# Splitting the selection over experts in two halves, moving the label row's product into the v product, and taking the low part of the log gates forward

## The reference

```
q2 = (x @ Wqa @ Wqb).reshape(B, L, H, DK) * scale
k2 = softmax((x @ Wka @ Wkb).reshape(B, L, H, DK), axis=-1)
gk1 = (log_sigmoid(x @ Wg1a @ Wg1b + bg1) / NORMALIZER).reshape(B, L, H, DK)
gk2 = (log_sigmoid(x @ Wg2a @ Wg2b + bg2) / NORMALIZER).reshape(B, L, H, DK)
e = softmax(x @ We, axis=-1)
_, idx = lax.top_k(e, 1)
mask = one_hot(idx, N_EXP).sum(-2)          # one expert per row
...
o_dense = gla_b(q1, k1, v, gk1)
o_sparse = gla_be(q_e, k_e, v, gk_e).sum(axis=1)
o = o_dense + o_sparse                      # gla: chunks of 64 rows, a running state per head
```

## Time and profile before

| | |
|---|---|
| median of 3 runs | 2540.27 us (2538.45 to 2542.61) |
| the profiled execution's own time | 2541.0 us |
| its span, first to last instruction | 2539.2 us |
| second pass, start of one step's `cumulate` to the next | 30.32 us |
| TensorE busy | 95% of the span |
| VectorE busy | 70% of the span |

### The profile page before, as it was taken

The page is one execution under the profiler, slowest core; times in us unless marked ns, Lnnn a source line. Parts: engine busy times, 40 slices in busy tenths (PEclk is TensorE's granted clock), DMA queues, the critical chain, the costliest instruction groups (busy, mean ns, idle before and its releaser), DMA issues.

```text
span 2539.2 us, 56360 instructions
## 1 busy us (share of the span) xinstructions
PE 2412.6 (95%) x20208; PEld 1423.8 (56%) x20208; DVE 1770.0 (70%) x3484; ACT 1562.6 (62%) x3281; POOL 1194.1 (47%) x929
## 2 busy tenths in 40 slices
PE   4999999998999999999999999999999999999997
PEld 2444444454666565666666665656666666666554
DVE  4444544426777777777777777777777777777775
ACT  3222323236777777777776777777777767777763
POOL 1797332214444444445544454444454444444444
PEclk9999999999999999999999999999999999999999
DMA  6434444311111111111111111111111111111111
GB/s 215 103 100 131 102 106 108 83 49 32 43 45 41 41 41 41 41 45 46 45 45 42 45 42 42 41 41 41 45 45 49 42 44 43 41 41 41 41 25 34
DMA packets 250704, 145.65 MB, mean 57 GB/s; under 512 B 208096, under 2 KB 208096, under 8 KB 250144
## 3 DMA queue, kind: packets, MB, share of 16 engines
q1 hardware_dynamic: 240048, 119.32, 18.8%
q10 hardware_dynamic: 9504, 17.31, 1.8%
q0 software_dynamic: 1104, 8.40, 0.9%
HBM read 61.09 MB, written 33.55 MB: 37 GB/s over the span
## 4 chain that ended last, share of the span: by engine, by line
PE 79%; DVE 13%; issue 4%; POOL 3%; DMA 1%; ACT 1%; DVEq 0%; POOLq 0%; SPq 0%; ACTq 0%
PE psum L319 17%; PE psum L320 16%; PE psum L321 16%; PE psum L583 6%; DVE region L1217 6%; PE psum L447 5%; PE psum L437 4%; PE psum L464 4%; PE psum L331 2%; DVE region L1214 2%; PE psum L456 2%; PE psum L418 2%; PE psum L367 1%; PE psum L419 1%; PE psum L368 1%
## 5 line engine op out<-in xcount | busy, mean ns | idle before, releaser
L1053 POOL TENSOR_TENSOR region<-region,kfac 128x512 f32<-128x512 f32 x64 | 124.4, 1944 | 379.4 <-DVE kfac L1304 379.4
L319 PE MATMUL psum<-wb,region 128*128 128x512 f16 x768 | 293.1, 382 | 0.0
L320 PE MATMUL psum<-wb,region 128*128 128x512 f16 x768 | 292.1, 380 | 0.0
L321 PE MATMUL psum<-wb,region 128*128 128x512 f16 x768 | 292.1, 380 | 0.0
L1036 POOL TENSOR_TENSOR region<-region 128x1024 f32<-128x1024 f32 x64 | 147.8, 2310 | 266.0 <-DVE region L1408 233.3
L1408 DVE SCALAR_TENSOR_TENSOR region<-psum,region 128x512 f16<-128x512 f32 x64 | 44.3, 692 | 225.3 <-ACT region L865 225.3
L1041 POOL TENSOR_TENSOR region<-region 128x1024 f32<-128x1024 f32 x64 | 150.8, 2356 | 105.3 <-DVE region L1183 105.3
L1048 POOL TENSOR_SCALAR region<-region,m 128x512 f32<-128x512 f32 x256 | 172.4, 693 | 34.8 <-DVE hm L1254 34.8
L583 PE MATMUL psum<-region 128*128 128x512 f16 x768 | 176.2, 379 | 2.1 <-DVE region L1408 2.1
L1081 POOL TENSOR_TENSOR og<-og 128x512 f16<-128x512 f32 x64 | 74.1, 1158 | 190.9 <-ACT og L807 190.9
L1217 DVE SCALAR_TENSOR_TENSOR region<-psum,m,region 128x512 f32<-128x512 f32 x192 | 144.2, 751 | 6.8
(11 more groups left out here) (232 smaller groups left out, 7204.2 us busy)
## 6 DMA issues: line engine op xcount, KB each, us to landing
region<-x_in SPq DMA_DIRECT2D x128, 256.0 KB, 2.6
q_cols<-region ACTq DMA_DIRECT2D x64, 256.0 KB, 2.5
region<-q_cols SPq DMA_DIRECT2D x64, 256.0 KB, 2.8
out_rows<-region SPq DMA_DIRECT2D x62, 256.0 KB, 2.0
region<-wb_in POOLq DMA_DIRECT2D x1, 3072.0 KB, 11.6
region<-wqkv_in SPq DMA_DIRECT2D x4, 512.0 KB, 6.0
region<-region SPq DMA_TRANSPOSE x128, 3.0
region<-ws_in POOLq DMA_DIRECT2D x1, 1280.0 KB, 15.7
```

Source lines behind the costliest of these rows:

```text
L319: mm(out, lhs(0), rhs(0), start=start, stop=False)
L320: mm(out, lhs(0), rhs(1), start=False, stop=False)
L321: return mm(out, lhs(1), rhs(0), start=False, stop=stop)
L1053: nc.gpsimd.tensor_tensor(kd.rearrange("p (h d) -> p h d", h=H2), kd.rearrange("p (h d) -> p h d", h=H2), kfac[:, :].unsqueeze(2).to_broad ...
```

## The change

Three edits, all in the second pass.

1. `back_select` works on heads 4 to 7 first and then on heads 0 to 3: eight operations of 128x256 in place of four of 128x512. `inter_sparse` signals after each half of its products, `project_k2` and `project_k`, which write banks 3 and 2, wait for the first half of the selection only, and `den` and `cumulate`, which write banks 0 and 1, for both.
2. `label_bc` is issued inside `project_v`, ahead of its last three products.
3. `front_kfac` is cut in two: its reduction `front_ksum` stays, then comes `front_lslow`, and the reciprocal and the scaling come behind it.

```diff
@@ tensor
-                    pe.wait_ge(S("sel_ok"), (n - 3) * 4 + 4)
+                    pe.wait_ge(S("sel_ok"), (n - 3) * 8 + 8)
...
-            def project_v(n):
+            def project_v(n, first):
                 pe.wait_ge(S("carry1_ok"), prev(n))
-                wide(n, 1, 2 * C, "v_pe")
+                for g in range(KT):
+                    last = mm3(bank[1], lambda x: xnT[:, x, g, :], lambda x: wb[:, x, g, 2 * C:], g == 0, g == KT - 1)
+                    if g == KT - 2:
+                        if first:
+                            pe.wait_ge(S("x1_ok"), cur(1))
+                        label_bc(n)
+                last.then_inc(S("v_pe"), 1)
...
             def project_k2(n, back):
                 pe.wait_ge(S("carry_ok"), prev(n))
                 if back:
-                    pe.wait_ge(S("sel_ok"), (n - 1) * 4 + 4)
+                    pe.wait_ge(S("sel_ok"), (n - 1) * 8 + 4)
...
             def project_k(n, back):
                 pe.wait_ge(S("ldiff_ok"), cur(n))
                 if back:
-                    pe.wait_ge(S("sel_ok"), (n - 1) * 4 + 4)
+                    pe.wait_ge(S("sel_ok"), (n - 1) * 8 + 4)
...
             def cumulate(n, back):
                 pe.wait_ge(S("v_ok"), cur(n))
                 if back:
-                    pe.wait_ge(S("sel_ok"), (n - 1) * 4 + 4)
+                    pe.wait_ge(S("sel_ok"), (n - 1) * 8 + 8)
...
@@ inter_sparse
-                last.then_inc(S("ix_pe"), 1)
+                    last.then_inc(S("ix_pe"), 1)
...
@@ vector, back_select
-                dve.wait_ge(S("ix_pe"), cur(n))
-                to = osum.rearrange("p (h d) -> p h d", h=H2)
                 of = psum[:, 0:4, :].rearrange("p b (r e d) -> p (b r) e d", r=2, e=NEXP)
-                ve.tensor_scalar(to, of[:, :, 0, :], m4[:, p, 0:1], None, ALU.mult).then_inc(S("sel_ok"), 1)
-                for e in range(1, NEXP):
-                    dve.wait_ge(S("sel_ok"), n * 4 + e)
-                    ve.scalar_tensor_tensor(to, of[:, :, e, :], m4[:, p, e:e + 1], to, ALU.mult, ALU.add).then_inc(S("sel_ok"), 1)
+                for done, half in enumerate((1, 0)):
+                    dve.wait_ge(S("ix_pe"), n * 2 + done + 2)
+                    to = osum.rearrange("p (h d) -> p h d", h=H2)[:, 4 * half:4 * half + 4]
+                    part = of[:, 4 * half:4 * half + 4]
+                    ve.tensor_scalar(to, part[:, :, 0, :], m4[:, p, 0:1], None, ALU.mult).then_inc(S("sel_ok"), 1)
+                    for e in range(1, NEXP):
+                        dve.wait_ge(S("sel_ok"), n * 8 + done * NEXP + e)
+                        ve.scalar_tensor_tensor(to, part[:, :, e, :], m4[:, p, e:e + 1], to, ALU.mult, ALU.add).then_inc(S("sel_ok"), 1)
...
-            def front_kfac(n):
+            def front_ksum(n):
                 dve.wait_ge(S("ke_ok"), cur(n))
                 ve.reduce_sum(ksum[:, :], heads(kd), X).then_inc(S("ksum_ok"), 1)
+
+            def front_kfac(n):
                 dve.wait_ge(S("ksum_ok"), n + 1)
...
                 if front:
+                    front_ksum(n)
+                    front_lslow(n)
                     front_kfac(n)
-                    front_lslow(n)
                     front_sil(n, p, tail)
```

More of the change, by code:

```diff
@@ L520, in step @@
                 if front:
[L521 to L524, removed]
+                    project_v(n, first)
                 if back:
@@ L1210, in back_select @@
                 dve.wait_ge(S("on_ok"), prev(n))
-                dve.wait_ge(S("ix_pe"), cur(n))
-                to = osum.rearrange("p (h d) -> p h d", h=H2)
                 of = psum[:, 0:4, :].rearrange("p b (r e d) -> p (b r) e d", r=2, e=NEXP)
-                ve.tensor_scalar(to, of[:, :, 0, :], m4[:, p, 0:1], None, ALU.mult).then_inc(S("sel_ok"), 1)
-                for e in range(1, NEXP):
-                    dve.wait_ge(S("sel_ok"), n * 4 + e)
-                    ve.scalar_tensor_tensor(to, of[:, :, e, :], m4[:, p, e:e + 1], to, ALU.mult, ALU.add).then_inc(S("sel_ok"), 1)
+                for done, half in enumerate((1, 0)):
[6 more added lines that the diff above has]
+                        ve.scalar_tensor_tensor(to, part[:, :, e, :], m4[:, p, e:e + 1], to, ALU.mult, ALU.add).then_inc(S("sel_ok"), 1)
             def back_join(n):
                 dve.wait_ge(S("o_pe"), cur(n))
-                dve.wait_ge(S("sel_ok"), n * 4 + 4)
+                dve.wait_ge(S("sel_ok"), n * 8 + 8)
                 ve.tensor_tensor(osum, bank[7], osum, ALU.add).then_inc(S("osum_ok"), 1)
```

## The result

The change made the kernel slower: 2561.53 us median (2560.68 to 2562.46, 4 runs) against 2540.15 us, a ratio of 1.0079 with a 95% interval of 1.0066 to 1.0092. The forecast was 2536 us. The profiled execution took 2561.3 us.

The account below looks back on a forecast made before the run. It took VectorE's path to the gates' low part, which `cumulate` on TensorE awaits, as the bound. Terms -0.47 + 0.86 - 0.46 = -0.07 us a step gave -4 us, about 2536 us against the median; 8 in 10 range 2522 to 2545.

Parts of the forecast that it names:

- What bounds the kernel: Second pass: `cumulate` on TensorE waits for VectorE's low part of the gates (L1285), by 0.3 us a step.
- TensorE's wait alone counts: At L418, TensorE's own waits hold it, so 0.61 us ahead of L367 come back: 37 us, 2503 us; chance 0.05.
- Term 1, the label square: Label square ahead of three v products: VectorE's wait at L1266 goes altogether, -0.47 us a step.
- Term 2, the selection: On VectorE, eight half-size operations replace four: 3.89 us against 3.03, +0.86 us a step.
- cheaper halves: Selection operations cost as little as L1230: -0.56 us a step, 34 us in all, 2507 us; chance 0.13.
- halves without overlap: Selection's halves cost the upper bound +1.09 us: step +0.16 us, +10 us, 2550 us; chance 0.10.
- Term 3, the low part: Low part of the gates directly behind kfac's reduction on VectorE: starts at 1528.87 instead of 1529.33, -0.46 us a step.
- The sum: Three terms on VectorE's path, -0.47 + 0.86 - 0.46 = -0.07 us a step, -4 us over 60 or so steps.
- The slower rival: Selection on VectorE: halves that do not overlap, step +0.16 us, +10 us, 2550 us; chance 0.10.

Follow-up runs that it names:

- lslow_only: Kernel before with only the low part of the gates moved in front of kfac's reciprocal and scaling: 2518.7 us, ratio 0.9911 to before.
- split_only: Kernel before with only the selection split into two halves, with all its waits: 2601.5 us, ratio 1.0235 to before.
- label_only: Kernel before with only the label square issued inside the v product: 2533.2 us, ratio 0.9966 to before.
- after_moved: Changed kernel with the one-hot marks issued between the two groups of masked scores, when GpSimd is idle: 2538.2 us, ratio 0.9987 to before.
- after_am_short: Changed kernel with GpSimd's addition of masked scores done for even heads only (results differ from the reference): one run, 2539.0 us.
- no_split: Changed kernel with the selection left unsplit, label square and low part still moved: 2513.0 us, ratio 0.9885 to before.

## Why the prediction was wrong

**What bounds the kernel: right.** `cumulate` stood behind the low part of the gates, and TensorE's wait at L367 was upstream of it. `lslow_only` gained 0.89% with that wait untouched, `split_only` lost 2.35% with it removed. The rival that TensorE's wait alone counts is refuted by both. In the first step of the pass the trace of before even names what it leaves unnamed later:

```profile
PE psum L418 <- DVE region L1285: 4.9, 1, 4.9
```

One reading was wrong there without harm: the 57 waits of the earlier trace rows are not all of the pass with some records missing. The rows are those from 780 us on, the pass starts near 570 us, and over the whole of it L1266 has 64 executions. The figures per step are the same.

**Term 1, the label square: the step that failed.** I wrote that the wait at L1266 "goes altogether" and took -0.47 us for the path, with all that follows L1266 moved forward unchanged. The wait did go: 22.3 us of idle time ahead of L1266 in the earlier trace rows are 0.1 us now, as the last number of this group says.

```profile
L1271 DVE SCALAR_TENSOR_TENSOR same_d<-psum,lab,cst 128x128 f16<-128x128 f32 x56 | 19.2, 342 | 0.1
```

But the marks, which the sum did not touch, took 0.56 - 0.23 = 0.33 us more, so that 0.14 of the 0.47 us reached the selection; `label_only`, all in all, gained 0.16 us a step. I followed the path along VectorE's own operations and their semaphores and asked for nothing else that could hold an instruction whose semaphores were all there. The rows of GpSimd around the place, which I had in front of me and did not use, show an addition that ends 0.04 us before the marks start. Any forward move of the marks had to run into it, short of one to before its start, as in `after_moved`.

The same interaction the other way round was in the trace of before, on GpSimd. Its multiplication by kfac, before, after, and in `lslow_only`:

```profile
L1053 POOL TENSOR_TENSOR region<-region,kfac x64: 1940/1942/2067, 584.5 to 2498.2; 128x512 f32<-128x512 f32 x64
```

```profile
L1056 POOL TENSOR_TENSOR region<-region,kfac x64: 1041/1042/1044, 589.9 to 2521.8; 128x512 f32<-128x512 f32 x64
```

```profile
L1053 POOL TENSOR_TENSOR region<-region,kfac x64: 1041/1042/1044, 589.8 to 2479.1; 128x512 f32<-128x512 f32 x64
```

Before, it started while VectorE ran L1285, 128x1024 with both inputs in SBUF, to 1530.55, and took 0.90 us more:

```profile
1529.51 1.94 POOL L1053 TENSOR_TENSOR region<-region,kfac 128x512 f32<-128x512 f32 x1 [5.93 <-DVE kfac L1304]
```

With the low part moved, kfac comes behind that operation, and the multiplication is at its own length. It takes 1.94 us in all three runs with the low part in its old place (before, `label_only`, `split_only`) and 1.04 in the ten others. The Trainium skill, SBUF — State Buffer, section on SBUF's two separate sides, states the rule: VectorE and GpSimd share one pair of ports, which is locked for a whole instruction, and a VectorE operation with two SBUF inputs (against a GpSimd operation that reads SBUF), or in a two-port mode, takes part in that lock. The runs agree, for the 0.33, 1.61 and 1.80 us that the held operations took more, for the 0.90 us on GpSimd, and for L1273, which was not held. That the one-input form of the marks is in such a mode is what the page would make of it; the runs show only that it is held like the two-input form.

**Term 2, the selection: right.** Forecast 3.89 us, measured 3.91; operations of 484 and 479 ns where the line through 128 and 512 elements gave 479:

```profile
L1222 DVE SCALAR_TENSOR_TENSOR region<-psum,m,region 128x256 f32<-128x256 f32 x336 | 162.6, 484 | 12.0
...
L1219 DVE TENSOR_SCALAR region<-psum,m 128x256 f32<-128x256 f32 x112 | 53.7, 479 | 1.8
```

`split_only` puts the edit at +0.865 us a step. The cheaper halves did not come, and neither did halves without overlap: the second half's L1219 starts at 1351.24, 0.08 us before the first half ends, and so does L1263 behind the second.

**Term 3, the low part: right.** -0.47 us from the reduction to its start, against -0.46. GpSimd's idle time took the later kfac.

**The sum.** With 0.33 us put in, -0.07 + 0.33 = +0.26 us a step, or 16 us over 60 steps; measured, 30.667 - 30.375 = 0.29 us over 63 steps, 18.4 us of the 21 between the medians. After_moved and after_am_short, without the hold, gave 2538.2 and 2539.0 us for a forecast of 2536. The slower rival had the right sign for another reason: I had looked for it in the fixed costs of the halves.

Two small things are open. In the second half of the pass every other step of the changed kernel is some 0.09 us longer than its neighbours, with VectorE starting L1178 that much later; the runs made from the whole change show it too, those with one edit alone and `no_split` don't. The products and the labels ahead of L1178 come at the same time in both. Its cause was not tested. And the profiled execution of before reached its first `cumulate` at 585.8 us, those of all other kernels between 587 and 591, though nothing in the first pass differs; this is some 4 us of the 20 between the two spans, and the runs' own spread is about as large.

## What to carry to other kernels

Before moving an operation on VectorE forward, lay GpSimd's timeline beside it: an operation whose data all lies in SBUF may not be able to run where its semaphores let it. The sign is one that now starts within some hundredths of a microsecond behind the end of a GpSimd operation: moved forward a little, it falls inside it. A wait on the busiest engine is worth only what the next wait behind it leaves; ask which of the two is last, and move that one's operation (0.9% here for swapping two lines). And cutting an operation to release its reader sooner costs the path another fixed part per piece, here 0.22 us each (0.88 us for four); do it only where the reader, and not the cutting engine, is last.

## What the runs showed of the hardware

- An operation of 128x4 or 128x8 on VectorE with its inputs in SBUF lasted until a GpSimd operation on SBUF that was under way had ended: 0.56, 1.78 and 2.03 us in place of 0.17 to 0.23. The profile books the time as busy and names no releaser, so VectorE's busy time in the changed kernel holds some 64 x 0.33 = 21 us of such holding.
- With the tensor in PSUM the same operation took 0.21 us beside the same GpSimd operation. A per-row factor from SBUF did not matter there.
- The other way round, GpSimd's multiplication of 128x512 took 1.94 us when it started beside a VectorE operation with two SBUF inputs, and 1.04 us otherwise.
- Dependent operations on VectorE stand 0.035 us apart and independent ones overlap by 0.08 us, for 128x256 as for 128x512.
